# An attention block's output projection in f32r parts, in a kernel of attention and mixture of experts on Trainium2

## What is computed

```python
P = X @ W_in + b_in                      # Q, K, V, G for 16 heads of 64
Q, K, V, G = jnp.split(P, splits, axis=-1)
W = jnp.power(EPS + _cdist(Q, K), -P_POW)            # P_POW = 2
W = W / (EPS + jnp.sum(W, axis=-1, keepdims=True))
A = jnp.einsum('hbts,hbse->hbte', W, V)
H = G * A
H = jnp.transpose(H, (1, 2, 0, 3)).reshape(b, t, HEADS * DIMS[2])
return H @ W_out + b_out                 # the output projection: 1024 x 128
...
x = x + _L0_attn_ref(_layernorm(x, axis=-1), ...)
x = x + _L0_ffn_ref(_layernorm(x, axis=-1), ...)     # the experts
```

## Time and profile before

| | |
|---|---|
| median of 3 runs | 1419.25 us (1418.08 to 1421.17) |
| the profiled execution | 1417.84 us, its span 1416.1 us |
| TensorE matmuls busy | 98% of the span |
| ScalarE busy | 78% |
| VectorE busy | 77% |
| GpSimd busy | 59% |
| DMA queue of the kernel | 13.0% of 16 engines' span |
| granted TensorE clock, mean | 0.997 |

### The profile page before, as it was taken

One profiled execution on the slowest core, in us unless ns is written; L12 is line 12 of the kernel. 1 busy time (PEld: TensorE's weight loads), 2 busy tenths in 40 slices (PEclk: granted clock), 3 DMA queues, 4 the chain that ended last, 5 costly groups with the idle time before them and its releaser, 6 DMA issues.

```text
span 1416.1 us, 18228 instructions
## 1 busy us (share of the span) xinstructions
PE 1385.1 (98%) x6488; PEld 742.1 (52%) x6488; DVE 1091.4 (77%) x2045; ACT 1099.4 (78%) x947; POOL 840.5 (59%) x657
## 2 busy tenths in 40 slices
PE   8999999999999999999999999899999999999996
PEld 4444444444444444444444444445777777777775
DVE  7887897788888887887888778635687686776857
ACT  2799789979978979979979979944676676766761
POOL 4568777777778778868877877411333333434330
PEclk9999999999999999999999999999999999999999
DMA  3000110111101101101101012443011010110100
GB/s 114 1 17 16 31 39 17 23 31 32 25 16 46 24 17 36 34 17 31 39 16 32 16 25 58 124 143 107 1 68 56 12 68 1 68 61 8 68 1 16
DMA packets 45705, 54.99 MB, mean 39 GB/s; under 512 B 13808, under 2 KB 32368, under 8 KB 44464
## 3 DMA queue, kind: packets, MB, share of 16 engines
q1 hardware_dynamic: 45616, 53.84, 13.0%
HBM read 48.97 MB, written 4.85 MB: 38 GB/s over the span
## 4 chain that ended last, share of the span: by engine, by line
PE 86%; DVE 8%; ACT 5%; issue 1%; DMA 0%; POOL 0%; SPq 0%; DVEq 0%; POOLq 0%
PE sc L406 14%; PE av L419 13%; PE z L74 12%; PE pj L74 12%; PE y L1214 8%; PE sc L401 6%; PE y L74 5%; PE pj L383 4%; PE pj L451 4%; DVE w L597 3%; PE pj L429 2%; ACT w L684 1%; ACT w L688 1%; ACT w L680 1%; DVE high L565 1%
## 5 line engine op out<-in xcount | busy, mean ns | idle before, releaser
L597 DVE TENSOR_SCALAR w<-sc 128x1024 f32<-128x1024 f32 x256 | 301.3, 1218 | 67.7 <-PE sc L406 66.4
L680 ACT ACTIVATE w<-w 128x2048 f32<-128x2048 f32 x128 | 237.6, 1904 | 121.5 <-DVE w L597 121.2
L320 POOL TENSOR_TENSOR wsum<-wsum,w 128x512 f32<-128x512 f32 x248 | 318.0, 1282 | 19.4
L969 POOL TENSOR_TENSOR hr_l<-hr,hr_h 128x512 fp32r<-128x512 f32 x112 | 151.9, 1357 | 261.6 <-ACT hr L1025 261.6
L406 PE MATMUL sc<-query,key 64*128 64x512 f32 x1024 | 241.7, 591 | 0.0
L684 ACT ACTIVATE w<-w 128x2048 f32<-128x2048 f32 x128 | 240.1, 1899 | 0.4
L688 ACT ACTIVATE w<-w 128x2048 f32<-128x2048 f32 x128 | 239.8, 1897 | 0.0
L419 PE MATMUL av<-w,vt 128*64 128x512 f32 x1024 | 233.8, 598 | 2.5 <-ACT w L688 2.4
L1025 ACT ACTIVATE hr<-z,b 128x512 f32<-128x512 f32 x256 | 173.4, 684 | 67.7 <-PE z L74 67.7
L306 POOL TENSOR_TENSOR sqq<-query 128x512 f32<-128x512 f32 x63 | 65.6, 1042 | 182.8 <-DVE query L537 137.1
L317 POOL TENSOR_TENSOR wsum<-w 128x512 f32<-128x512 f32 x124 | 159.3, 1285 | 5.2 <-ACT w L688 5.2
(11 more groups left out here) (214 smaller groups left out, 2360.7 us busy)
## 6 DMA issues: line engine op xcount, KB each, us to landing
hT<-head_recips SPq DMA_DIRECT2D x64, 256.0 KB, 4.0
rb<-routing SPq DMA_DIRECT2D x8, 2048.0 KB, 7.1
w<-in_W SPq DMA_DIRECT2D x16, 256.0 KB, 5.4
xa<-in_X SPq DMA_DIRECT2D x8, 256.0 KB, 4.4
xc<-in_X SPq DMA_DIRECT2D x8, 256.0 KB, 2.8
x<-xc SPq DMA_DIRECT2D x8, 256.0 KB, 4.1
x<-x SPq DMA_DIRECT2D x1, 1792.0 KB, 7.9
out<-prod SPq DMA_DIRECT2D x7, 256.0 KB, 2.3
```

The source lines that it names most:

```text
L320: nc.gpsimd.tensor_tensor(wsum[:, u, :], wsum[:, u, :], w[:, j % 2, u, c, :], ALU.add).then_inc(s_added, 1)
L597: nc.vector.tensor_scalar(w[:, s, 2 * r:2 * r + 2, c, :], sc[:, i, :, :], 0.0, None, ALU.max).then_inc(s_d2, 1)
L680: nc.scalar.activation(w[:, j % 2, u, :, :], w[:, j % 2, u, :, :], ACT.Sqrt).then_inc(s_sqrt, 1)
```

## The change

The output projection goes over to f32r parts. The weights `wout` are split once into a high and a low part (ScalarE copies in round 1, GpSimd subtracts in round 3). `hT` is split each quad: ScalarE's `high_part` copies it into `hT_h` ahead of the third square root of round j (for quad j - 3), GpSimd's `low_part` subtracts between the two pairs of squares of the next round, and for the last three quads GpSimd's `last_parts` makes both. `output` has six matmuls instead of two: first the four with the high part of `hT` (by both parts of the weights), then, behind a wait for `s_hT_l`, two with its low part. It now stands one round later (quad j - 4), and `turn_output`, `add_output`, `store_x1` and `load_x(xc)` move to rounds with q = 3. GpSimd's `normalize` moves from the start of round j to the end of round j - 1. SyncE waits for the output of quad j - 2 before it spreads the reciprocals into `hT`. To make room, `xs` and `krow` keep one buffer instead of two, and the tiles of `build_rest` are laid out in another order. In the passage one output more comes after the attention loop, and the steps are moved as the diff shows; the routing weights of the last two experts are loaded by a DMA of their own; the split of the experts' second weights starts four steps later, and TensorE waits for it expert by expert. Left out of the diff here: the new tiles and semaphores, the indices of `xs` and `krow`, the two lines where the functions are handed on, and the wait for `rb_late` in `weigh`.

```diff
-            if k == 1 and 0 <= j - 3 < NQ:
-                names.append(("out", j - 3))
-            if k == 2 and q == 2 and b >= 1:
+            if k == 1 and 0 <= j - 4 < NQ:
+                names.append(("out", j - 4))
+            if k == 2 and q == 3 and b >= 1:
...
+                if j >= 2:
+                    sp.wait_ge(s_pj, use["out", j - 2] + 1)
...
-                if q == 0 and b >= 1:
+                if q == 2 and b >= 1:
                     store_x1(b - 1)
                     load_x(xc, b, s_xc)
...
+            def low_part(j):
+
+                pool.wait_ge(s_hT_h, j + 1)
+                nc.gpsimd.tensor_tensor(hT_l[:, j % 2, :, :], hT[:, j % 2, :, :], hT_h[:, :, :].bitcast(F32),
+                                        ALU.subtract).then_inc(s_hT_l, 1)
+
+            def last_parts(j):
+
+                pool.wait_ge(s_hT, j + 1)
+                pool.wait_ge(s_pj, use["out", j - 1] + 1)
+                nc.gpsimd.tensor_copy(hT_h[:, :, :], hT[:, j % 2, :, :]).then_inc(s_hT_h, 1)
+                low_part(j)
+
             for j in range(-1, NQ):
-                if 0 <= j - 3 < NQ:
-                    normalize(j - 3)
                 if j + 1 < NQ:
                     squares(j + 1, 0)
+                    if j == 3:
+                        pool.wait_ge(s_wout, 1)
+                        nc.gpsimd.tensor_tensor(wout[1][:, :, :], wout_f[:, :, :], wout[0][:, :, :].bitcast(F32),
+                                                ALU.subtract).then_inc(s_wout, 1)
+                    if 0 <= j - 4:
+                        low_part(j - 4)
                     if j >= 0:
                         squares(j + 1, 1)
+                elif j == NQ - 1:
+                    low_part(j - 4)
                 if j == -1:
                     for k, (source, hi, lo) in enumerate(weights_to_split()[1:]):
                         pool.wait_ge(s_rest_h, k + 1)
                         nc.gpsimd.tensor_tensor(lo, source, hi.bitcast(F32), ALU.subtract).then_inc(s_rest_l, 1)
-                if 0 <= j - 1 < NQ:
-                    for u in range(4):
+                for u in range(4):
+                    if 0 <= j - 1 < NQ:
                         add_chunks(j - 1, u)
-            return normalize
+                if 0 <= j - 2 < NQ:
+                    normalize(j - 2)
+            return normalize, low_part, last_parts
...
-                    pe.wait_ge(s_late_in, 16 * N_LATE)
-                if j == NQ - 3:
-                    fill(nc, pj[:, n, :], ident, 4)
-                pe.wait_ge(s_hT, j + 1)
+                    pe.wait_ge(s_wout, 2)
+                pe.wait_ge(s_hT_h, j + 1)
                 for r in range(2):
-                    m = nc.tensor.matmul(pj[:, n, :], wout[:, 2 * (j % QUADS) + r, :], hT[:, j % 2, r, :],
-                                         start=(r == 0), stop=(r == 1))
+                    for i in range(2):
+                        nc.tensor.matmul(pj[:, n, :], wout[i][:, 2 * (j % QUADS) + r, :], hT_h[:, r, :],
+                                         start=(r + i == 0), stop=False)
+
+                pe.wait_ge(s_hT_l, j + 1)
+                for r in range(2):
+                    m = nc.tensor.matmul(pj[:, n, :], wout[0][:, 2 * (j % QUADS) + r, :], hT_l[:, j % 2, r, :],
+                                         start=False, stop=(r == 1))
                 m.then_inc(s_pj, 1)
...
+            def high_part(j):
+                act.wait_ge(s_hT, j + 1)
+                if j >= 1:
+                    act.wait_ge(s_pj, use["out", j - 1] + 1)
+                nc.scalar.copy(hT_h[:, :, :], hT[:, j % 2, :, :]).then_inc(s_hT_h, 1)
+
             def square_roots(j):
                 for u in range(4):
                     r, v = divmod(u, 2)
+                    if u == 2 and j == 1:
+                        act.wait_ge(s_late_in, 16 * N_LATE)
+                        nc.scalar.copy(wout[0][:, :, :], wout_f[:, :, :]).then_inc(s_wout, 1)
+                    if u == 2 and j >= 3:
+                        high_part(j - 3)
                     act.wait_ge(s_d2, 8 * j + 4 * r + 4)
                     nc.scalar.activation(w[:, j % 2, u, :, :], w[:, j % 2, u, :, :], ACT.Sqrt).then_inc(s_sqrt, 1)
...
+                    sp.dma_start(rb0[:, 0:NE - 2, :], rwd[0, 0:NE - 2].partition_broadcast(P)).then_inc(S["rb"], 16)
...
+            store_x1(B - 2)
+            load_xc(B - 1)
             normalizer(NQ - 2)
             spread_routing(0)
             sp.wait_ge(att["pj"], use["sum", NQ - 1] + 1)
             sp.wait_ge(att["gated"], 2 * NQ)
+            sp.dma_start(rb0[:, NE - 2:, :], rwd[0, NE - 2:].partition_broadcast(P)).then_inc(S["rb_late"], 16)
...
-            normalize(NQ - 3)
+            normalize, low_part, last_parts = att_gpsimd(pool)
+            low_part(NQ - 4)
+            last_parts(NQ - 3)
             normalize(NQ - 2)
+            last_parts(NQ - 2)
             normalize(NQ - 1)
+            last_parts(NQ - 1)
             pool.wait_ge(att["x1_out"], 16 * B)
...
-                if n == NU + 1:
-                    pe.wait_ge(S["w2s"], NE * NF)
+                if b == 1 and i == 1:
+                    pe.wait_ge(S["w2s"], NF * (k // NF + 1))
...
                 if (b, k) == (0, 3):
                     last_sums()
-                if (b, k) == (0, 7):
+                if (b, k) == (0, 4):
+                    output(NQ - 3)
+                if (b, k) == (0, 10):
                     output(NQ - 2)
-                if (b, k) == (0, 16):
+                if (b, k) == (0, 19):
                     output(NQ - 1)
-                if (b, k) == (0, 18):
+                if (b, k) == (0, 22):
                     turn_output(B - 1)
...
             sums(NQ - 2)
-            output(NQ - 3)
...
+                if n == 4:
+                    output(NQ - 4)
...
                 if (b, k) == (0, 4):
                     weighted_values(NQ - 1, 1)
                     sums(NQ - 1)
+                if (b, k) == (0, 5):
+                    output(NQ - 3)
+                if (b, k) == (0, 4):
                     for e in range(5, NE):
                         split_w1(e)
                 if (b, k) == (0, 8):
+                    dve.wait_ge(S["in_b2"], 16)
+                if (b, k) == (0, 11):
+                    reciprocals(NQ - 1)
+                if (b, k) == (0, 12):
                     output(NQ - 2)
-                    dve.wait_ge(S["in_b2"], 16)
-                if (b, k) == (0, 12):
-                    reciprocals(NQ - 1)
-                if (b, k) == (0, 20):
+                if (b, k) == (0, 22):
                     output(NQ - 1)
-                if (b, k) == (0, 21):
+                if (b, k) == (0, 24):
                     add_output(B - 1)
-                if b == 0 and k >= 24:
-                    if k == 24:
+                if 28 <= n < 28 + NE:
+                    if n == 28:
                         dve.wait_ge(att["x1_out"], 16 * B)
-                    dve.wait_ge(in_w2[k - 24], 16)
-                    split_w2(k - 24)
+                    dve.wait_ge(in_w2[n - 28], 16)
+                    split_w2(n - 28)
...
             reciprocals(NQ - 2)
+            output(NQ - 4)
```

68 lines of the change are left out of this document (39 added, 29 removed).

## The result

The changed kernel takes 1427.56 us in the median of 6 runs (1425.91 to 1428.19), the kernel before 1418.31 us beside it (1417.50 to 1421.17). The ratio is 1.0059 with an interval of 1.0048 to 1.0070: slower by 0.6%, where 0.6% faster had been predicted. The span of the profiled execution grew from 1416.1 to 1424.8 us.

What follows compares the result with a forecast made beforehand. TensorE, with 86% of the chain of waits, was taken as the bound. Attention's 10.7 us gain less 2.4 lost at the passage took 1417.84 to 1409.5; 1.4 for the timed median gave 1410.9, stated as 1411.0, range 1404 to 1417.

Steps and rivals of the forecast that it cites:

- the low part: GpSimd's subtraction between the squares: 2.37 us, ready 0.5 us before TensorE asks; nothing waits, no port block in the loop.
- largest delay seen, 0.5 us: Late-stage GpSimd subtraction into hr_l, 1291 ns median and 1812 at most: taken as the limit of port delay.
- The output in f32r: Attention loop, slot 1: six f32r matmuls at 1.47 us for 1.80, gaining 0.33 us in 27 quads, 8.8 us.
- ScalarE's copy: high_part ahead of the third square root: 0.95 us inside a gap of 1.11, so no cost in the loop.
- the first rival: ScalarE takes the gain back: 1453 us if its copy needs table changes, 1431 if the gap can't be filled; 6%.
- The second rival: The low part comes late through the port rule and TensorE waits in mid-group: some 1430 us; 3%.
- The transpose of the output: Moved from third to fourth quad: 0.59 us gained against 0.45 lost per batch, 1.3 us gained in all.
- The loop in sum: Attention stage: 8.8 + 0.6 + 1.3 = 10.7 us gained.
- The passage: From attention to the experts: 1.0 + 0.6 + 0.2 - 1.4 + 2.0 = 2.4 us lost.
- the wait of 2.0 us for the routing weights: At turn_routing(1) TensorE stalls because add_output precedes ranks and routing on VectorE: +2.0 us, bounds 0 and 2.5.
- "0 to 1 us, I take 0.2" for turn_f(1): In the passage TensorE may wait for VectorE, whose statistics now stand behind output(NQ - 2): 0.2 us lost.
- The sum: Whole kernel: -10.7 + 2.4 = -8.3 us, giving 1411.0 us, 0.6% faster.

Runs made afterwards that it cites:

- e9_full_wait_between: e7 with the wait for the low part between the two f32 products instead of ahead of the first: 1420.25 us, ratio 1.0005.
- e7: e3_both with the output projection as two f32 products of the high parts, the wait for the low part ahead of both: 1428.43 us, ratio 1.0061.
- e10: e3_both with the wait for the low part and its two products ahead of the four high-part products: 1418.05 us, ratio 0.9993.
- e6: e3_both with ScalarE making the high-part copy twice in 27 quads: 1413.20 us, ratio 0.9952.
- e3_both: The changed kernel with the edits of e1_low_first and e2 together: 1412.24 us, ratio 0.9954.
- e1_low_first: The changed kernel with GpSimd's low_part ahead of the first pair of squares in rounds with q = 2: 1416.97 us, ratio 0.9992.
- e2: The changed kernel with GpSimd waiting in the passage for VectorE's xn_f ahead of low_part(NQ - 4) and normalize(NQ - 1): 1419.65 us, ratio 1.0009.
- e4_order: e3_both with normalize(NQ - 3) also behind the first xn_f and add_output moved to VectorE's step 27: 1408.13 us, ratio 0.9929.

## Why the prediction was wrong

The step that failed stands in the part on the low part: "By the rule there is thus no block in the loop; one block of 0.5 us would just use up the 0.5 us of cover". The rule of the Trainium skill ("SBUF — State Buffer", section "Who interferes with whom") was weighed in one direction only: whether VectorE could hold up GpSimd's new subtraction. The ports are held by whoever has them, and the runs show it the other way round: GpSimd's new instruction holds up VectorE's old ones. And the list of VectorE's instructions in that stretch (`w<-sc`, `query`, `key`, all from PSUM) left out `norm_apply`, four instructions from on-chip memory to on-chip memory that stand there in one quad of four. Each new GpSimd instruction should have been set against every such instruction of VectorE in its stretch. By the row in the trace of before (0.34 us free, 0.82 when it met a square of 1.04 us and ended with it) the price could have been worked out: for VectorE the full 2.4 us. It even stood there at full length. The instructions of `xn_f` in the trace of before:

```profile
L743 DVE TENSOR_SCALAR xn_f<-x_first,mv_f,rstd_f x4: 331/334/2164, 903.4 to 906.0; 128x128 f32<-128x128 f32 x4
```

The 2.16 us lie beside GpSimd's product `hT` of 2.38 us. So the prediction's "largest delay seen, 0.5 us" was taken from GpSimd's rows alone (`hr_l`), and its sentence "The trace and the Trainium skill differ here" doesn't hold: the trace of before agreed.

Point by point:

- **The output in f32r**, 0.33 us a quad: right, 5.68 to 5.35 us in the trace; 0.33 in e9_full_wait_between. Its place in time too: e7 and e10 show that, in the rounds with q = 0 and 3, the low part comes 0.4 us after TensorE has reached the output, and four products of 0.23 us cover it with the half microsecond to spare that was forecast.
- **ScalarE's copy**: right. It took 1.03 us, costs nothing in the loop, and could be twice as long there in rounds 5 to 30 (e6). It needs no change of table either side, so the first rival is out.
- **The low part**: wrong as told. Its effect on who waits for it was right (nobody), its effect on who shares its port was missed: 9.6 us in the loop. The second rival had the mechanism with the victims exchanged, at 3%.
- **The transpose of the output**: right by its parts, with -0.59 us in slot 2 of the rounds with q = 2 (e3_both; in the changed kernel the block covers it) and +0.43 to 0.46 in those with q = 3, where 0.45 was forecast.
- **The loop in sum**: 10.7 us forecast; e1_low_first is 9.9 us ahead at the start of round 30 and 10.65 at the start of round 31, the changed kernel 0.15 behind and 0.6 ahead. In round 3 the gain was 0.7 us, with 0.6 forecast.
- **The passage**: 2.4 us lost by forecast, 9.4 measured, 1.6 with GpSimd out of the way (e2). Right in it were the wait of 2.0 us for the routing weights (1.91 in the trace, and gone in e4_order) and the wait of 1.42 us in the earlier trace rows that went. "0 to 1 us, I take 0.2" for turn_f(1) was a wait of 3.70 us. The +1.0 us of ScalarE's copy is there too: its four square roots took 7.30 us before and 8.25 with the copy between them. The copy of 128x1024 on GpSimd, bounded by 1.0 and 2.4, took 1.04 us. That the clock could fall, to 1.2 GHz for 10.2 and 3.4 us, was in no step at all.
- **The sum**: 1411.0 us forecast, 1412.24 for the change without its collisions (e3_both), 1427.56 with them.

What isn't settled: why the clock falls behind some waits of 1.9 to 2.7 us and not behind others of the same length (see the last section), and so how much of the first 2.6 us lost at the passage is clock and how much wait.

## What to carry to other kernels

Before work is put on GpSimd, list what VectorE does in that stretch that reads and writes on-chip memory without PSUM, the forms of the last section above all. VectorE loses the new instruction's full length there, whoever waits for its result, and TensorE what is left of it behind the slack (0.84 us in this loop). The same work a few microseconds earlier or later can be free, as e1_low_first and e4_order show: they are 9.5 and 18 us faster than the changed kernel with the same instructions at other places. Products that need no late operand go first: that saved 0.63 us a time here in half the rounds. And in a trace, a form that takes 0.33 us in the median and 2.16 at most, as `xn_f` did before the change, has met something; ask what, before adding more of it.

## What the runs showed of the hardware

- GpSimd's tensor_tensor and its copy stop VectorE's tensor_scalar with one input and its tensor_tensor with two, both from on-chip memory to on-chip memory, until they have ended (tensor_scalar ends 0.08 us later): 0.34 us becomes 2.44 beside 2.41 us of GpSimd, 1.93 beside 1.89, 2.43 beside 2.39; 1.18 beside the copy of 1.04; a subtraction of 0.69 us becomes 2.73. The Trainium skill ("SBUF — State Buffer", section "Who interferes with whom") calls the shared port pair an exclusive lock, and the trace agrees for the direction in which GpSimd holds it. VectorE's instructions that take the scores from PSUM aren't touched: `w<-sc` has a mean of 1217 ns after the change.

```profile
L633 DVE TENSOR_SCALAR w<-sc 128x1024 f32<-128x1024 f32 x256 | 301.0, 1217 | 63.4 <-PE sc L438 62.6
```

- Not all that goes from on-chip memory to on-chip memory is held: VectorE's statistics (BATCH_NORM_STATS2) of 128x128 took 0.27 to 0.29 us wherever they stood, also wholly inside a subtraction of GpSimd's. VectorE and GpSimd after the change:

```profile
882.83 0.66 DVE L777 BATCH_NORM_STATS2 stats_f<-x_first 128x6 f32<-128x128 f32 x3
```

```profile
882.24 2.38 POOL L343 TENSOR_TENSOR hT_l<-hT,hT_h 128x1024 fp32r<-128x1024 f32 x1
```

- GpSimd's tensor_tensor of 128x1024 took 1.89 us with one tile for both operands and 2.39 us with two.
- Six f32r products take 0.33 us less than two f32 ones of the same size in the same slot.
- TensorE's clock fell to 0.50 (1.2 GHz) about waits of 3.9 and 3.7 us in a stretch where it was busy otherwise, and stayed there for 10.2 and 3.4 us; in e2_passage it stayed there for 6.8 us behind a wait of 1.89, in e4_order for 3.4 us each behind waits of 2.0 and 2.59. The length of the wait doesn't decide it: behind waits of 1.91 and 1.96 us in the changed kernel and one of 3.02 in e6_copy_twice it stayed at 1.00, as it did behind all waits of the passage before, up to 1.66 us.
- A fall of 3.4 us with TensorE busy costs 1.6 to 1.7 us: 1.6 in e3_both at turn_routing(1), and 1.7 in round 0, where every run has the same wait of 2.50 us for `krow` and the clock fell behind it in the profiled executions of e6, e9 and e10 alone. Ends of spans can thus differ by 1.7 us between executions for no reason in the edit.
